# Block-sparse attention: pairs of PSUM banks exchanged, VectorE's work beside projections, products with v of two quarters in two pieces each

## The reference, cut to what matters

```python
BLOCK_SIZE, GLOBAL_EVERY = 128, 24
bi = jnp.arange(seq_len) // BLOCK_SIZE
is_global = bi % GLOBAL_EVERY == 0
allowed = (bi[:, None] == bi[None, :]) | is_global[:, None] | is_global[None, :]
mask = jnp.where(allowed, 0.0, -jnp.inf)
qkv = x @ w_qkv.T + b_qkv
scores = jnp.einsum('bhqd,bhkd->bhqk', q * scale, k) + mask
attn = jax.nn.softmax(scores, axis=-1)
out = jnp.einsum('bhqk,bhkd->bhqd', attn, v)
return out.transpose(0, 2, 1, 3).reshape(B, L, D) @ w_out.T + b_out
```

## Time and profile before

| | before |
|---|---|
| median of 3 runs | 3181.27 us |
| the profiled execution: time, span | 3180.86 us, 3179.1 us |
| TensorE, VectorE, ScalarE, GpSimd busy, share of the span | 94%, 73%, 54%, 54% |
| block-sparse stage, about | 1276 to 1756 us of the span |

### The profile page before, as it was taken

One profiled execution on the slowest core, in us unless ns is written; L12 is line 12 of the kernel. 1 busy time (PEld: TensorE's weight loads), 2 busy tenths in 40 slices (PEclk: granted clock), 3 DMA queues, 4 the chain that ended last, 5 costly groups with the idle time before them and its releaser, 6 DMA issues. The chain is left out here.

```text
span 3179.1 us, 46100 instructions
## 1 busy us (share of the span) xinstructions
PE 2984.7 (94%) x14188; PEld 1732.9 (55%) x14188; DVE 2335.8 (73%) x4188; ACT 1701.7 (54%) x3501; POOL 1715.9 (54%) x1118
## 2 busy tenths in 40 slices
PE   6999999999999988899999799999999999999997
PEld 2454545454545444455555466666666666666665
DVE  8999999999999989577775655556666555565553
ACT  4777686868586853344444344444444444444442
POOL 2666666666666655233433455555555555565552
PEclk9999999999999999899999799999999999999998
DMA  4757675767666665311010000000001200000000
GB/s 142 259 210 263 213 252 215 249 215 249 222 240 232 231 218 202 113 41 35 31 33 28 21 20 20 0 20 20 20 20 40 74 21 19 20 26 26 26 13 21
DMA packets 131300, 343.37 MB, mean 108 GB/s; under 512 B 14898, under 2 KB 57990, under 8 KB 131222
## 3 DMA queue, kind: packets, MB, share of 16 engines
q1 hardware_dynamic: 128918, 334.02, 30.6%
q10 hardware_dynamic: 2304, 8.39, 0.7%
HBM read 320.87 MB, written 21.50 MB: 108 GB/s over the span
## 5 line engine op out<-in xcount | busy, mean ns | idle before, releaser
L559 POOL TENSOR_TENSOR hb<-bcB,du 128x1024 f32<-128x1024 f32 x256 | 602.1, 2352 | 391.6 <-DVE hb L699 348.7
L688 DVE TENSOR_TENSOR_SCAN ps_dA<-ps_dA,hb 128x1024 f32<-128x1024 f32 x256 | 585.7, 2288 | 44.2 <-ACT ps_dA L914 44.2
L1226 PE MATMUL ps_y<-hb,ident 128*128 128x512 f32 x1024 | 491.6, 609 | 28.0 <-DVE hb L699 27.9
L2339 POOL TENSOR_TENSOR c_pr<-c_pr,c_inv 128x512 f32<-128x512 f32 (+1 forms) x256 | 236.9, 933 | 322.0 <-DVE c_inv L2460 322.0
L914 ACT ACTIVATE ps_dA<-delta,a_neg 128x511 f32<-128x511 f32 x512 | 330.1, 676 | 1.1
L1226 PEld LDWEIGHTS ps_y<-hb,ident 128*128 128x128 f32 x1024 | 189.9, 193 | 250.5 <-issue 187.2
L699 DVE TENSOR_TENSOR hb<-ps_dA,bcC 128x1024 f32<-128x1024 f32 x256 | 311.8, 1218 | 5.9
L2598 ACT ACTIVATE c_pr<-c_ps_s,c_negmax 128x256 f32<-128x256 f32 (+1 forms) x512 | 223.5, 451 | 147.4 <-DVE c_negmax L2453 124.4
L1769 ACT ACTIVATE b_pt<-b_ps_t 128x512 f32<-128x512 f32 x320 | 174.1, 595 | 208.6 <-PE b_ps_t L1889 207.7
L2453 DVE CUSTOM_DVE_ANT_0 c_ps_s<-c_ps_s,c_mask 128x256 f32<-128x256 f32 (+1 forms) x512 | 188.4, 418 | 120.3 <-issue 120.3
L2316 POOL TENSOR_TENSOR c_q_cos<-c_q_cos,c_q_sin 128x1024 f32<-128x1024 f32 x60 | 141.5, 2358 | 232.1 <-DVE c_q_sin L2425 230.3
(11 more groups left out here) (312 smaller groups left out, 5896.2 us busy)
## 6 DMA issues: line engine op xcount, KB each, us to landing
bcB<-bc_scratch SPq DMA_DIRECT2D x256, 512.0 KB, 4.4
bcC<-bc_scratch SPq DMA_DIRECT2D x256, 512.0 KB, 4.6
c_x<-stream_scratch SPq DMA_DIRECT2D x16, 512.0 KB, 5.0
c_xr<-stream_scratch SPq DMA_DIRECT2D x16, 512.0 KB, 3.6
rows<-in_x_dram SPq DMA_DIRECT2D x8, 512.0 KB, 5.3
sum<-in_x_dram SPq DMA_DIRECT2D x8, 512.0 KB, 7.8
x_scratch<-sum SPq DMA_DIRECT2D x8, 512.0 KB, 6.8
b_xb<-x_scratch SPq DMA_DIRECT2D x8, 512.0 KB, 4.6
```

Source lines behind the costliest of these rows:

```text
L559: pool.tensor_tensor(hb[:, s % RING, :, :], bcB[:, s % ROWS, :, :], bc(du[:, c % 2, :].unsqueeze(1), [P, NG, T]), ALU.mult)\
L688: dve.tensor_tensor_scan(flat(h_all), flat(h_all), flat(tile), 0.0, ALU.mult, ALU.add)\
L1226: last = pe.matmul(ps_y[:, :], W["ident"][:, :], hb[:, r % RING, i, :], start=False, stop=(g == GROUPS - 1 and i == NG - 1))
L2339: pool.tensor_tensor(rows, rows, bc(inv[:, u, :].unsqueeze(2), [P, 2, w]), ALU.mult)\
```

## The change

The pairs of set 0 are exchanged in `pair_of`, and what followed from them with it: `score` of (n, 0) at k8 and k9 of the first half goes to pair 0, the turned maxima of set 1 to bank 2, v and the output projection to banks 2 and 3. The waits at k8 ask for one maximum fewer. VectorE's reciprocals move to k4 and k5 of both halves, `statistics` to the first half's k9 ahead of `add_rows`, `norm` to the second half's k5. GpSimd's `root` moves to behind `add_bias`. `weigh` of quarter 1 is cut into a piece after k4 and one after k5, that of quarter 3 into a piece after k8 and one after k9; its count is raised by the last piece. In the order of the code, the piece stands ahead of `turn_x`, `project_v` and, in k5, of `project_qk`, and in k9 ahead of `project_out`.

```diff
--- before.py
+++ after.py
@@ -1398,7 +1398,7 @@
 
         def pair_of(m, k):
 
-            return (1, 1, 0, 1, 0, 1, 0, 1, 0, 1)[k] if m else (1, 1, 1, 0, 1, 0, 1, 1, 0, 1)[k]
+            return (1, 1, 0, 1, 0, 1, 0, 1, 0, 1)[k] if m else (0, 0, 0, 1, 0, 1, 0, 0, 1, 0)[k]
 
         def attended(ap, blk):
 
@@ -1555,12 +1555,12 @@
                 if more:
                     mask(n, 0, 1, USES, b)
                 add_bias(b)
+                if more2:
+                    root(n + 1)
                 if more:
                     place_v(n, 0)
                     mask(n, 1, 0, USES, b)
                 divide(b, 0)
-                if more2:
-                    root(n + 1)
                 part_out(b, 1)
                 if more:
                     mask(n, 1, 1, USES, b)
@@ -1629,7 +1629,7 @@
                 dve.wait_ge(max_turned.s, max_turned.at(n, m + 1))
                 dve.wait_ge(masked.s, masked.at(n, 2 * m + 2))
                 for e in range(2):
-                    dve.scalar_tensor_tensor(qa[:, m, e, :], ps_s[:, 0, :], ones_row[:, e:e + 1], qa[:, m, e, :],
+                    dve.scalar_tensor_tensor(qa[:, m, e, :], ps_s[:, 2 * m, :], ones_row[:, e:e + 1], qa[:, m, e, :],
                                              ALU.mult, ALU.add).then_inc(qa_ready.s, 1)
 
             def take_second_out(b, m):
@@ -1655,13 +1655,13 @@
             def take_v(n):
                 dve.wait_ge(v_proj.s, v_proj.at(n, 1))
                 dve.wait_ge(v_ready.s, v_ready.at(n, 0))
-                dve.tensor_copy(v_rows[:, :, :], ps_s[:, 0:2, :].rearrange("p a (t d) -> p (a t) d", t=2)).then_inc(v_taken.s, 1)
+                dve.tensor_copy(v_rows[:, :, :], ps_s[:, 2:4, :].rearrange("p a (t d) -> p (a t) d", t=2)).then_inc(v_taken.s, 1)
 
             def add_rows(b):
                 dve.wait_ge(xb_ready.s, xb_ready.at(b, 1))
                 dve.wait_ge(stored.s, stored.at(b, 0))
                 dve.wait_ge(out_done.s, out_done.at(b, 1))
-                dve.tensor_tensor(res[:, :, :], ps_s[:, 0:2, :].rearrange("p a (t d) -> p (a t) d", t=2), xb[:, :, :], ALU.add)\
+                dve.tensor_tensor(res[:, :, :], ps_s[:, 2:4, :].rearrange("p a (t d) -> p (a t) d", t=2), xb[:, :, :], ALU.add)\
                     .then_inc(res_ready.s, 1)
 
             def first():
@@ -1685,7 +1685,7 @@
                     elif more:
                         maximum(b + 1, 0, k + 2, pair_of(0, k + 2))
                 elif more:
-                    maximum(b + 1, m, k - 8, 1)
+                    maximum(b + 1, m, k - 8, m)
 
             def body(b, prev, more, more2):
                 n = b + 1
@@ -1694,26 +1694,26 @@
                     if prev:
                         if k == 0:
                             take_second_out(b - 1, 1)
-                        if 2 <= k <= 5:
-                            invert(b - 1, 1, k - 2)
+                        for part in {4: (0,), 5: (1, 2, 3)}.get(k, ()):
+                            invert(b - 1, 1, part)
                     if k == 8:
                         add_maxima(b, 1)
+                    if more2 and k == 9:
+                        statistics(n + 1)
                     if prev and k == 9:
                         add_rows(b - 1)
                 for k in range(GROUPS):
                     half(b, 1, k, more)
                     if k == 0:
                         take_second_out(b, 0)
-                    if 1 <= k <= 4:
-                        invert(b, 0, k - 1)
+                    for part in {4: (0, 1), 5: (2, 3)}.get(k, ()):
+                        invert(b, 0, part)
                     if more and k == 4:
                         take_v(n)
                     if more2 and k == 5:
-                        statistics(n + 1)
+                        norm(n + 1)
                     if more and k == 8:
                         add_maxima(n, 0)
-                    if more2 and k == 9:
-                        norm(n + 1)
 
             def last(b):
                 cols = lambda t: slice(t * P, (t + 1) * P)
@@ -1847,7 +1847,7 @@
             def project_v(n):
                 for t in range(TT):
                     for k in range(DC):
-                        last = pe.matmul(ps_s[:, t // 2, t % 2 * D:t % 2 * D + D], xT[:, k, t * P:(t + 1) * P],
+                        last = pe.matmul(ps_s[:, 2 + t // 2, t % 2 * D:t % 2 * D + D], xT[:, k, t * P:(t + 1) * P],
                                          w_qkv[:, k, 2 * D:3 * D], start=(k == 0), stop=(k == DC - 1))
                 last.then_inc(v_proj.s, 1)
 
@@ -1895,10 +1895,10 @@
 
                 pe.wait_ge(max_ready.s, max_ready.at(n, m * GROUPS + GROUPS))
                 for t in range(TT):
-                    last = pe.transpose(ps_s[:, 0, t * P:(t + 1) * P], negmax[:, m, t, :], ident[:, :])
+                    last = pe.transpose(ps_s[:, 2 * m, t * P:(t + 1) * P], negmax[:, m, t, :], ident[:, :])
                 last.then_inc(max_turned.s, 1)
 
-            def weigh(b, m, i, uses, b_used):
+            def weigh(b, m, i, uses, b_used, pieces=(0, 1)):
 
                 pe.wait_ge(emptied.s, used(b_used, uses["p", m, 2 * i + 1, 1]))
                 if i == 0:
@@ -1910,6 +1910,8 @@
                 if i == 3:
                     work.append((2, 1))
                 for n, (q, c) in enumerate(work):
+                    if n not in pieces:
+                        continue
                     e, blk = PARTS[q][c]
                     w = T // len(PARTS[q])
                     for g in range(G):
@@ -1917,13 +1919,14 @@
                                          shaped(pt[:, q % SLOTS, g, c * w:(c + 1) * w], blk),
                                          start=(i in (0, 3) and n == 0), stop=(i in (2, 4) and n == len(work) - 1),
                                          skip_group_check=True)
-                last.then_inc(pv_done.s, 1)
+                if len(work) - 1 in pieces:
+                    last.then_inc(pv_done.s, 1)
 
             def project_out(b):
                 pe.wait_ge(oT_ready.s, oT_ready.at(b, DC))
                 for t in range(TT):
                     for k in range(DC):
-                        last = pe.matmul(ps_s[:, t // 2, t % 2 * D:t % 2 * D + D], oT[:, k, t * P:(t + 1) * P], w_o[:, k, :],
+                        last = pe.matmul(ps_s[:, 2 + t // 2, t % 2 * D:t % 2 * D + D], oT[:, k, t * P:(t + 1) * P], w_o[:, k, :],
                                          start=(k == 0), stop=(k == DC - 1))
                 last.then_inc(out_done.s, 1)
 
@@ -1960,15 +1963,17 @@
                             pe.wait_ge(max_ready.s, max_ready.at(b, GROUPS + k + 1))
                         score(b, 1, k + 2, pair_of(1, k + 2))
                     elif more:
-                        pe.wait_ge(max_ready.s, max_ready.at(b, 2 * GROUPS) if k == 8 else max_ready.at(n, 1))
-                        score(n, 0, k - 8, 1)
+                        pe.wait_ge(max_ready.s, max_ready.at(b, 2 * GROUPS - 1) if k == 8 else max_ready.at(n, 1))
+                        score(n, 0, k - 8, 0)
                     score_keys(b, 0, k, uses)
                     if prev and k == 0:
                         weigh(b - 1, 1, 4, USES, b - 1)
                     if k == 8:
                         turn_maxima(b, 1)
-                    if k in (2, 4, 6, 8):
+                    if k in (2, 6):
                         weigh(b, 0, (k - 2) // 2, uses, b)
+                    if k in (4, 5, 8, 9):
+                        weigh(b, 0, k // 4 * 2 - 1, uses, b, (k % 4,))
                     if more and k in (3, 4):
                         for h in (2 * (k - 3), 2 * (k - 3) + 1):
                             turn_x(n, h, b, uses["x", h])
@@ -1988,7 +1993,7 @@
                         elif k == 6:
                             pe.wait_ge(v_taken.s, v_taken.at(n, 1))
                         elif k == 8:
-                            pe.wait_ge(max_ready.s, max_ready.at(n, GROUPS))
+                            pe.wait_ge(max_ready.s, max_ready.at(n, GROUPS - 1))
                         elif k == 9:
                             pe.wait_ge(max_ready.s, max_ready.at(n, GROUPS + 1))
                         elif k == 0:
@@ -2008,8 +2013,10 @@
                         weigh(b, 0, 4, uses, b)
                     if more and k == 8:
                         turn_maxima(n, 0)
-                    if k in (2, 4, 6, 8):
+                    if k in (2, 6):
                         weigh(b, 1, (k - 2) // 2, uses, b)
+                    if k in (4, 5, 8, 9):
+                        weigh(b, 1, k // 4 * 2 - 1, uses, b, (k % 4,))
                     if more and k == 4:
                         pe.wait_ge(max_ready.s, max_ready.at(n, 6))
                         project_v(n)
```

## The result

| | before | after |
|---|---|---|
| median of 5 runs each, in turn on one chip | 3181.64 us (3180.43 to 3183.82) | 3165.43 us (3162.87 to 3167.55) |
| ratio, with its 95% interval | | 0.9949 (0.9937 to 0.9961) |
| the profiled execution: time, span | 3180.86 us, 3179.1 us | 3163.27 us, 3161.5 us |
| one looped batch, from a turning of the maxima to the next (mean of four) | 56.88 us | 54.49 us |

The kernel is 16.2 us faster, 0.5%, and 3165.43 stands beside the forecast of 3165.0. The two profiled executions are 17.6 us apart: 16.2 of it between the stage's first and last turning of the maxima, and 0.7 each ahead of and behind these.

The account below looks back on a forecast made before the run. TensorE's order of work was taken to set the 56.90 us batch period, with waits for VectorE's maxima and a pair limit; terms summed to -2.49 a looped batch, -16.3 in all, giving 3165 us, range 3154 to 3175.

Parts of the forecast that it names:

- The second limit that no wait names: Two back-to-back groups on TensorE cost about 2.95 us, waiting for ScalarE to empty score banks, whatever VectorE's wait.
- Rival 1: The pair is no limit, so every VectorE wait goes at full length: 4.1 us a batch, 3154 us; chance 0.13.
- Pairs of banks: k7 and k8 of both halves fall from 3.83 to 2.95 us once k8's wait goes: -1.76 us a looped batch.
- The slack that I worked out: Margin of 0.4 us by which k7's maximum should be ready before TensorE reaches the turning of the maxima.
- rival 3: The turning of the maxima takes over all of k8's wait, leaving 3176 us; chance 0.05.
- Norm and reciprocals: VectorE's norm leaving second-half k9 shortens w0 to k3, -0.58 us; moving reciprocals to k4-k5 gives -0.05 a looped batch.
- rival 4: Slower: norm in second-half k5 waits for rstd behind b_xb's DMA, example 3187 us; chance 0.03, 0.05 with unknown mishaps.
- The price of a piece: Each added piece of the quarter 1 and 3 products costs TensorE about 0.14 us, four times: +0.55 a looped batch.
- rival 2: Added pieces cost up to 0.57 us each, 2.3 a batch instead of 0.55: 3173 to 3176 us; chance 0.13.
- What the pieces buy: Quarter 3's second piece between k9 and next k0 turns 2.93 us into 1.08 + about 1.2: -0.65 a looped batch.
- The stage's ends: Batches outside the five looped: first -1.2 us, seventh -1.9, last -0.8; with the loop's -12.4, -16.3 together.
- the signs that were named: Trace signs: period 54.4 us, no wait before k8, k7 with k8 2.95, pieces 0.57, w0 to k3 1.0.

Follow-up runs that it names:

- run 1: Exchange of the pairs of banks alone, with the banks and waits that go with it, on the kernel before: period 55.10 us against 56.88, median 3170.46 us, ratio 0.9968.
- run 12: The changed kernel with the eight reciprocals of a batch put back among k1 to k5: period 54.59 us, median 3164.00 us, ratio 0.9946 against before.
- runs 5: The changed kernel with a useless ScalarE copy ahead of the first exponential of k1 and k7, both halves: period 55.59 us, median 3180.84 us.
- run 6: The changed kernel with four useless ScalarE copies a batch at groups that have a projection behind them: period 54.49 us, median 3167.07 us.
- run 2: The kernel before with VectorE's and GpSimd's moves alone (norm, statistics, root, reciprocals): period 56.28 us, median 3178.58 us, ratio 0.9992.
- run 7: The changed kernel with quarter 1's products in one piece again, quarter 3's still in two: period 54.21 us, median 3171.05 us.
- run 4: The changed kernel with the products of quarters 1 and 3 whole again: period 54.51 us, median 3168.00 us, ratio 0.9964 against before.
- run 3: The kernel before with only the products of quarters 1 and 3 cut in two pieces: period 56.95 us, median 3186.04 us, ratio 1.0005.
- run 8: The changed kernel with quarter 1's second piece, in the second half all its products, between k7 and k8: period 53.21 us, median 3162.69 us.
- run 10: Quarter 1's products late, between k7 and k8, plus useless matmuls in the last half, on the changed kernel: period 53.21 us, median 3157.29 us.
- run 9: The changed kernel with useless score matmuls in the last batch's second half: period 54.49 us, median 3166.25 us, ratio 0.9955 against before.

## Why the prediction was right, point by point

- **The second limit that no wait names.** It carried the prediction, and it was right: every pair of after takes 2.94 to 2.96, without any wait in it. Rival 1 (waits go at full length, 3154) falls by run 1 (2.40 of waits for 1.78), run 12 (0.5 for 0.1) and the runs 5 and 6.
- **Pairs of banks**, -1.76: run 1 measured -1.78. The turning waits for nothing; VectorE waits 0.18 for it instead. The slack that I worked out (0.4) was enough, and rival 3 falls with that.
- **Norm and reciprocals**, -0.58 and -0.05: run 2 measured -0.60 together, run 12 has -0.10 for the reciprocals in after.
- **What norm could wait for** (rival 4): GpSimd did wait longer for the DMA, 9.0 against 8.4 us, and norm still found rstd ready. Covered, as costed.
- **The price of a piece**, 0.14: run 7 has 0.28 for two. The row of the short w2 was the right one to go by, and rival 2 falls: pieces behind groups whose banks are not empty take 0.57 as well (1491.47 to 1492.04). The Trainium skill, TensorEngine Tiling (Array Packing), Key Properties, has TensorE drain when the tiling mode changes; the trace agrees that an added piece costs something, and that whole something is 0.14 here; no run parts a drain from the rest of it.
- **What the pieces buy** is the term that was mis-sized. I had k9 alone at 1.08 and k0 at about 1.2, 0.65 gained. k9 does take 1.08, but k0 takes 1.28, and the three together come to 2.93, as long as the pair did before: the piece is hidden, and so the gain is the piece's own 0.57. With four pieces' price of 0.55 the whole part is worth 0.02 in a looped batch (runs 4 and 3: -0.02 and +0.07), not 0.10, and 1.2 in all at the two ends (run 4). The period is therefore 54.49, not 54.4.
- **The stage's ends.** My sum had 16.3 for the whole stage. By TensorE's timelines it is 16.3 from the first turning to the stage's last product (454.83, then 438.54), but 1.4 of that is the first half batch, which can't be told from the clock, so 14.9 is what the change itself is shown to give. Cut at the start of each first half's w4, so that the gain at a batch's start falls to the stretch before it, my terms are 1.85 for the first, 12.4 for the five looped, 1.9 for the seventh and 0.15 for the last. Measured are 1.35 (from its half's turning on), 11.8, 1.85, and a loss of 0.15. So the looped term was 0.1 a batch too hopeful, and the first and the last together 0.8. That 3165.43 came so near to 3165.0 is partly chance: the first half batch's 1.4 made up for what the other terms lack, and the runs of after spread over 4.7 us themselves.

All the signs that were named came: no wait before k8, 2.94 for k7 and k8, pieces of 0.57, 0.99 from w0 to k3, statistics before the output projection's end; k9 to the end of k0 was given as 2.85 and is 2.93.

## What to carry to other kernels

A named wait is worth only what it exceeds the next limit by; before costing its removal, find the same two instructions somewhere in the trace where the wait is absent, and take the difference. Where two groups back to back are held by the engine that empties their banks, put work between them that TensorE owes anyway (run 8: 1.28 us a batch), rather than splitting work where a long instruction already stands behind the group (w1 in the change: 0.28 lost). Read the steady period and the ends of a stage apart, since the granted clock at an end can take back what the loop gained.

## What was not expected of the hardware

**The clock at the stage's end.** Four profiled executions (runs 3, 5, 7, 8) had TensorE's granted clock at 0.5 to 0.7 in much of the last batch's second half, where before and after had 1.00, and lost 7 to 11 us of rest against before and after, though TensorE has the same products to make there. Shorter falls cost less: run 1 had 0.67 in 1730 to 1740, run 6 and run 9 had 0.66 in 1700 to 1710, with 1.8 to 2.5 us more of rest than after. That TensorE's idle gaps have a part in it is what run 10 shows: useless matmuls in them kept the clock at 1.00 up to 1720 (0.82 in the 10 us after) and gave 8.5 us of rest back, and each of its five runs lies under each of run 8's (3153.96 to 3157.87 against 3162.13 to 3164.26). What is not settled is why before and after keep it: in the 10 us ahead of the fall run 8 had TensorE busy for 8.96 (66 matmuls), and the stretch of after with 8.95 (78 matmuls, 1710 to 1720) was followed by 1.00. What tells the two apart was not tried. Nor does the code alone decide it, as run 9 beside after shows, so that the clock of one profiled execution doesn't stand for a kernel's: run 3's twelve runs fall into two groups. The spread of after's runs is not explained.

**Norm went from 1.75 to 1.28 us** with the same four instructions (the earlier trace rows and 1513.05 above). In its old place part of it ran beside GpSimd's work on the mask, in the new one GpSimd is idle. That this is the reason was only argued: no run moved GpSimd's work alone. As norm is covered, it is worth nothing here.
